# Latent attention: a turn in five runs of one array shape, the fifth chunk's scores in the next turn's first run, projections in the banks of the scores

## The reference

```python
# x: (4, 512, 128) normalised, ctx: (4, 77, 128); 16 heads of 64
q = norm_l(x) @ Wq                          # queries
k, v = split(concat(norm_x(x), ctx) @ Wkv)  # 512 + 77 keys
q, k = rmsnorm(q) * g_q, rmsnorm(k) * g_k   # over the 64 of a head
p = softmax(q @ k.T * 64 ** -0.5)           # masked context keys are left out
out = x + (p @ v) @ Wout + bout
```

## Time and profile before

| | |
|---|---|
| Median of 3 runs | 1910.01 us (1908.96 to 1915.94) |
| Profiled execution | 1905.26 us |
| Its span | 1903.4 us |
| Granted clock, mean of the span | 0.977 |
| PE busy | 1758.1 us (92%) |
| DVE busy | 1469.1 us (77%) |
| ACT busy | 1032.9 us (54%) |
| POOL busy | 701.0 us (37%) |

### The profile page before, as it was taken

The page is one execution under the profiler, slowest core; times in us unless marked ns, Lnnn a source line. Parts: engine busy times, 40 slices in busy tenths (PEclk is TensorE's granted clock), DMA queues, the critical chain, the costliest instruction groups (busy, mean ns, idle before and its releaser), DMA issues. The chain is left out here.

```text
span 1903.4 us, 29213 instructions
## 1 busy us (share of the span) xinstructions
PE 1758.1 (92%) x10747; PEld 1302.9 (68%) x10747; DVE 1469.1 (77%) x2712; ACT 1032.9 (54%) x1570; POOL 701.0 (37%) x571
## 2 busy tenths in 40 slices
PE   5998999689999999999989999899899999989898
PEld 4767888455555655555556777677558889957676
DVE  6887987767767767677668888799799955577798
ACT  3657878457776777767645555455300310055685
POOL 3643221144555555555430444364112302012231
PEclk9998999889999999999989999899999999999899
DMA  2001111100000000000001211000000010000032
GB/s 68 2 15 58 67 67 56 53 1 1 1 1 1 1 1 1 1 1 1 1 20 56 67 67 55 13 1 2 18 17 28 28 56 1 0 13 2 30 111 100
DMA packets 21191, 51.46 MB, mean 27 GB/s; under 512 B 3563, under 2 KB 11383, under 8 KB 18116
## 3 DMA queue, kind: packets, MB, share of 16 engines
q1 hardware_dynamic: 20596, 49.53, 7.6%
q10 hardware_dynamic: 464, 0.20, 0.1%
HBM read 48.48 MB, written 1.25 MB: 26 GB/s over the span
## 5 line engine op out<-in xcount | busy, mean ns | idle before, releaser
L1612 POOL TENSOR_TENSOR sb_L_total<-sb_L_total,sb_L_probT 128x512 f32<-128x512 f32 x128 | 161.4, 1293 | 170.8 <-ACT sb_L_probT L1949 170.8
L441 POOL TENSOR_TENSOR sb_L_prob<-sb_L_prob,sb_L_rsum 128x616 f32<-128x616 f32 (+1 forms) x96 | 105.6, 1121 | 226.3 <-DVE sb_L_rsum L743 226.3
L2017 DVE TENSOR_REDUCE sb_L_tops<-banks 128x2 f32<-128x1024 f32 x128 | 156.4, 1223 | 28.6 <-PE banks L1724 27.0
L1949 ACT ACTIVATE sb_L_probT<-banks 128x1024 f32<-128x1024 f32 x128 | 124.8, 1024 | 80.2 <-PE banks L1759 79.6
L1609 POOL TENSOR_TENSOR sb_L_total<-sb_L_probT 128x512 f32<-128x512 f32 x64 | 93.5, 1484 | 106.0 <-ACT sb_L_probT L1949 106.0
L1772 PE MATMUL banks<-sb_L_probT,sb_L_v 128*64 128x512 f32 x512 | 129.7, 608 | 0.0
L2399 DVE SCALAR_TENSOR_TENSOR sb_L2f_hid<-banks,sb_L2f_weight,sb_L2f_hid 128x512 f32<-128x512 f32 x176 | 122.1, 745 | 3.0 <-PE banks L97 1.6
L2469 DVE SCALAR_TENSOR_TENSOR sb_resid<-banks,sb_L2f_weight,sb_resid 128x128 f32<-128x128 f32 x192 | 67.2, 351 | 62.5 <-PE banks L97 57.9
L1315 DVE TENSOR_TENSOR sb_L0f_hid_low<-sb_L0f_raw,sb_L0f_hid_high 128x1024 fp32r<-128x1024 f32 x64 | 88.6, 1401 | 28.7 <-ACT sb_L0f_hid_high L1271 28.2
L1252 ACT ACTIVATE sb_L1f_gate<-banks 112x512 f32<-112x512 f32 x96 | 57.5, 599 | 91.1 <-PE banks L97 91.1
L529 PE MATMUL banks<-sb_ident,sb_L_prob 128*77 128x128 f32 x640 | 96.5, 284 | 5.8 <-POOL sb_L_prob L441 5.4
(11 more groups left out here) (433 smaller groups left out, 5321.9 us busy)
## 6 DMA issues: line engine op xcount, KB each, us to landing
sb_L0f_wide<-spread_L0f SPq DMA_DIRECT2D x7, 1024.0 KB, 7.7
sb_L1f_wide<-spread_L1f SPq DMA_DIRECT2D x7, 1024.0 KB, 7.3
sb_L3f_wide<-spread_L3f SPq DMA_DIRECT2D x7, 1024.0 KB, 4.8
sb_fetched<-L2f_w SPq DMA_DIRECT2D x12, 256.0 KB, 2.7
sb_fetched<-L1f_gu SPq DMA_DIRECT2D x8, 336.0 KB, 3.1
sb_fetched<-L0f_w SPq DMA_DIRECT2D x8, 259.0 KB, 2.8
sb_fetched<-L0f_w SPq DMA_DIRECT2D x8, 256.0 KB, 3.2
sb_normT<-L2f_w SPq DMA_DIRECT2D x2, 768.0 KB, 4.2
```

Of the source, the lines that this page charges most:

```text
L441: pool.tensor_tensor(grid, grid, bcast(rsum[:, n % PROBS, half], [None, KEYS]), ALU.mult).then_inc(normed, 1)
L1612: pool.tensor_tensor(sums, sums, probT[:, k, h], ALU.add).then_inc(added[h], 1)
L1949: act.activation(probT[:, k], ps[:, slot:slot + 2, :], ACT.Exp).then_inc(exped, 1)
L2017: dve.tensor_reduce(tops[:, :, k, 0], ps[:, banks:banks + 2, :], AX.X, ALU.max).then_inc(bound_read, 1)
```

## The change

The work stays the same, its order changes, and with the order the banks and the waits.

- TensorE's turn becomes: bound(0), scores(4) of the turn before, bound(1), scores(0), scores(1), bound(2) | product(2), product(3), product(4), SUM of the turn before | NKL, Q, V4, KL, a context projection or none, NQL | bound(3), scores(2), scores(3), bound(4) | product(0), MT, Y, product(1).
- Y is computed in two halves of 64 columns (shape 128x64): eight matmuls for four.
- KL, Q and V4 go to the banks of scores that have just been read; scores(2) and scores(3) then wait for their readers. Q is made three turns ahead instead of two, so `q_raw` has two buffers.
- ScalarE: `exps(turn - 1, 4)` begins the turn; the keys' root follows the inverse of the sum; `high_keys` stands ahead of exps(2), the queries' root between exps(2) and exps(3).
- VectorE: the reads of the bounds follow TensorE's order; `take_lead`, `scale_queries`, `add_result`, `low_queries` end the turn in this order.
- GpSimd: `low_keys` comes ahead of two additions.

```diff
@@ use_side
-                    if n >= len(EARLY) and kind not in ELSEWHERE:
-                        wait_read(pe, *last_beside(n))
-                    elif kind == KL and of == 3:
-                        wait_read(pe, KL, 2)
-                    elif kind == KL and of > 3:
-                        pe.wait_ge(mixed_ready, of - 3)
...
+                    if n >= len(EARLY):
+                        if kind == SUM and of + 2 < TURNS:
+                            pe.wait_ge(bound_read, (of + 2) * CHUNKS + 3)
+                        elif kind == NKL:
+                            wait_read(pe, *((NQL, of - 1) if of > 2 else (Q, 2)))
+                        elif kind == NQL:
+                            wait_read(pe, NKL, of)
+                        elif kind == KL and of > 2:
+                            pe.wait_ge(exped, (of - 3) * CHUNKS + 1)
+                        elif kind == Q and of > 2:
+                            pe.wait_ge(exped, (of - 3) * CHUNKS + 2)
+                        elif kind == V4:
+                            pe.wait_ge(exped, (of - 1) * CHUNKS + 2)
...
                         for t in range(TPB):
-                            last = pe.matmul(out[:, t * P:(t + 1) * P], mixedT[:, t * P:(t + 1) * P], wo[:, p, :], start=True, stop=True)
+                            for h in range(2):
+                                last = pe.matmul(out[HEAD[h], t * P:(t + 1) * P], mixedT[:, t * P + h * D:t * P + h * D + D], wo[:, p, :], start=True, stop=True)
@@ bound
                         if turn > 0:
                             wait_read(pe, MT, turn - 1)
-                    if k == 2 and turn > 0:
...
+                        if turn >= 3:
+                            wait_read(pe, Y, turn - 3)
+                    if k == 3 and turn > 1:
+                        wait_read(pe, SUM, turn - 2)
@@ scores
+                    if k == 2 and turn + 3 < TURNS:
+                        wait_read(pe, KL, turn + 3)
+                    if k == 3 and turn + 3 < TURNS:
+                        wait_read(pe, Q, turn + 3)
+                    if k == 3 and turn + 1 < TURNS:
+                        wait_read(pe, V4, turn + 1)
@@ ScalarE's turn
+                    if turn > 0:
+                        exps(turn - 1, 4)
                     exps(turn, 0)
                     exps(turn, 1)
...
+                        invert_sum(turn - 1)
+                        if much:
+                            invert_keys(turn + 2)
+                        if turn + 3 < TURNS:
+                            square_queries(turn + 3)
...
                     if much:
                         high_keys(turn + 2)
+                    exps(turn, 2)
+                    if much and turn > 0:
                         invert_queries(turn + 2)
-                    exps(turn, 4)
+                    exps(turn, 3)
```

189 lines of the change are left out of this document (103 added, 86 removed).

## The result

| | before | after |
|---|---|---|
| Median, each of 4 runs on the same chip | 1912.91 us (1908.96 to 1915.94) | 1931.58 us (1928.64 to 1934.57) |
| Profiled execution | 1905.26 us | 1928.64 us |
| Its span | 1903.4 us | 1926.8 us |
| PE busy | 1758.1 us | 1766.5 us |
| DVE busy | 1469.1 us | 1499.1 us |

The ratio is 1.0099, with an interval of 1.0070 to 1.0128: the change makes the kernel 1% slower, 18.7 us by the medians. The forecast was 1920, 10 us slower than the 1910.01 that it started from; the kernel before measured 1912.91 in the four runs beside the changed one.

What follows compares the result with a forecast made beforehand. TensorE's own stream was taken to set the time. About 29 turns at +0.39 us (+11.3) with the ends at -3 and +1.5 sum to +10: profiled 1905.26 becomes 1915, median 1920, range 1888 to 1934.

Steps and rivals of the forecast that it cites:

- likeliest case: Whole kernel: the forecast chain of waits closes, value 1920, own range 1914 to 1929; chance 0.50.
- Steps 1 and 2: Turn's start: bound(1) waits 0.55 us for VectorE's read of bound(0), starting at 1.83; bound(2) at 4.00, SUM at 6.98.
- Step 3: SUM to NQL: NQL at 11.3, its 0.44 us wait gone with a key-context projection (KC), about 0.55 without a context projection.
- Step 4: bound(3) to MT: without scores(4) between, MT starts 3.97 us after bound(3), at 15.87, and TensorE waits 0.26.
- Step 5: Turn's end: next bound(0) starts 2.60 us after MT, a wait of 0.56 in place of the hidden 0.20.
- The price of a change of shape: TensorE's array shape changes: a boundary is worth 0.18 to 0.2 us; removing two per turn saves 0.36 to 0.4.
- a matmul after a pause: TensorE after a wait: costs another 0.05 us or so per turn.
- The VC turn: Turn with the values' projection (VC), priced like V4 as half of 1.62 us: turn length 18.75 us.
- The ends: Stage's first and last turns: turn before last -3 us as moments move behind the last reduction; turn 0 +1.5.
- Rival 1 and 2: Both faster. First: fewer boundaries, no wait returns, 1875, chance 0.08. Second: only bound(1)'s 0.55 is real, 1891, chance 0.12.
- Rival 3: No change: the turn's tail releases bound(0) as now (0.20), 18.3 us per turn, 1908; chance 0.19.
- Rival 4: Slower still: ScalarE becomes late as well, 1930 to 1940; chance 0.11.

Runs made afterwards that it cites:

- scores_split: Changed kernel with the second half of scores(0) behind bound(1) and its first half ahead of it: 1923.60 us, ratio 1.0066 to the kernel before.
- fifth_home: Changed kernel with scores(4) back in its own turn behind bound(4), and scores(0) between bound(0) and bound(1): 1939.13 us, ratio 1.0144 to the kernel before.
- queries_first: Changed kernel with VectorE's scale_queries ahead of take_lead at the end of each turn: 1923.66 us, ratio 1.0058 to the kernel before.
- all_three_y_whole: Changed kernel with scale_context behind take_keys, scale_queries ahead of take_lead, scores(0) split around bound(1), and Y again as four 128x128 products: 1915.46 us, ratio 1.0026.
- two_more_bounds: Changed kernel with product(4) of the turn before moved from ahead of SUM to behind NKL, adding two shape changes: 1952.00 us, ratio 1.0219 to the kernel before.
- context_later: Changed kernel with VectorE's scale_context moved from ahead of part_key_squares to behind take_keys: 1925.56 us, ratio 1.0074 to the kernel before.
- gpsimd_add_later: Changed kernel with GpSimd's first addition of each turn moved behind low_keys: 1919.87 us, ratio 1.0042 to the kernel before.
- all_three_last: Changed kernel with scale_context behind take_keys, scale_queries ahead of take_lead, scores(0) split around bound(1), and the last turn's scores(4) ahead of product(0): 1906.85 us, ratio 0.9971.

## Why the prediction was right, and where it was not

The direction and its mechanism were right: TensorE loses two changes of shape in a turn and gets more in waits than it saves. The likeliest case's value was 1920 (its own range 1914 to 1929), the measured 1931.58 lies within the range of 1888 to 1934, near its upper end, and outside the likeliest case's own. The loss measured, 18.7 us, is nearly twice the 10 of the forecast, though the waits were where they were said to be. 2.9 of the 11.6 us between 1920 and 1931.58 are the kernel before, which measured that much above the 1910.01 of the forecast.

**Steps 1 and 2** held to 0.02 us (bound(1) 1.81 for 1.83, bound(2) 4.01 for 4.00, SUM 6.96 for 6.98). That bound(1) waits for VectorE and no longer for the stream is shown by scores_split, by fifth_home and by the 29 waits. They are named with 0.39 where 0.55 was forecast, which is the way of counting: by starts it is 0.58.

**Step 3** held: NQL 11.29 for 11.3. In turns without a projection its wait is 0.35 by name where 0.55 was forecast, but by starts it is 0.51 (L97 at 686.21, NQL at 686.95, and such a pass takes 0.23), and the turn is 18.55 for 18.5.

**Step 4** held: MT 15.92 for 15.87, 3.97 behind bound(3) to the digit. Its wait is not in the list; it shows only as 1.18 us from product(0) where 0.86 is work, 0.32 for 0.26.

**Step 5** held: bound(0) 2.63 us behind MT for 2.60. queries_first shows that the order of the two VectorE instructions is worth 0.3 us of the wait; the other 0.2 us end with Y's addition by the rows, which no run tests alone.

**The price of a change of shape** held: 0.19 us each (all_three_y_whole; about 0.16 in the KC turn of two_more_bounds) for 0.18 to 0.20. The "0.05 or so" for a matmul after a pause stands on no row, and no run here shows it by itself.

**The VC turn** is the term that was mis-sized. The prediction has it as "One with VC (like V4, half of the 1.62 from 691.21 to 692.83) 18.75"; it measured 19.62. 0.87 us in seven turns is 6.1 of the 6.8 us by which the 29 turns (+18.1 for +11.3) exceed the forecast. The walk through the KC turn was carried over to the VC turn with only TensorE's work changed. But in the VC turn VectorE has one instruction more, and the change moves it from the tail to ahead of the subtraction that NKL waits for; there it stands beside GpSimd's addition, and so does the subtraction behind it. "VectorE by then has read bound(1) and (2) and done the sum's tail; no wait" was true of KC alone. context_later and gpsimd_add_later each take these 0.8 us away, by different ends.

**The ends** were off in parts that nearly cancel: turn 0 -0.6 for +1.5, the turn before last -3.7 for -3, and +3.4 at the last turn, which the forecast did not have. all_three_last shows 2.0 of that to be the last scores; the rest stays open. That the ends sum to -0.9 for a forecast of -1.5 is luck. In turn 0 the clock differs as well: it stood at 0.50 from 398.1 to 404.7 in the kernel before and from 400.9 to 404.1 in the changed one; how much of the -0.6 that is stays open.

**Rivals.** Rival 1 and 2 fall with the waits. Rival 3 falls with step 5. Rival 4 had 1930 to 1940, where the time is, but by a cause that is not there: ScalarE took the queries' high part 0.04 us behind VectorE's scaling of them, as soon as this came earlier (queries_first). The lateness was VectorE's.

## What to carry to other kernels

Where two engines take turns at the same two banks, the reader's time spaces the writer's work, and joining runs of one shape can take away just the work that covered it; ask of each piece that is moved what it was covering. A walk through one kind of turn doesn't hold for the others: go through the instructions that only some turns have, on every engine. And when an instruction of VectorE with both inputs in SBUF takes far longer in one place than in another, look at what GpSimd does beside it, and at which of the two starts first, before moving anything on the busiest engine.
